# Batches in pairs: 32-row class products, a ring of seven PSUM banks, and fp16 row products in a fused layernorm and graph-convolution kernel

## What is computed

```python
def reference(x, adj, L0_gnn_b1, L0_gnn_b2):
    h = jnp.maximum(_layernorm(x, axis=-1), 0.0)
    return x + _L0_gnn_ref(h, adj, L0_gnn_b1, adj, L0_gnn_b2)

def _construct_adj(x, k):              # k = 8
    fv = x.mean(axis=1)
    nf = fv / jnp.linalg.norm(fv, axis=1, keepdims=True)
    sim = nf[:, :, None] * nf[:, None, :]
    _, idx = jax.lax.top_k(sim, k + 1)
    idx = idx[..., 1:]
    adj = jnp.zeros((Bn, Nn, Nn), x.dtype).at[b_ix, r_ix, idx].set(1.0)
    adj = jnp.maximum(adj, jnp.swapaxes(adj, 1, 2))
    return adj.at[:, d, d].set(1.0)

def _gc(x, adj, W, b):
    deg = adj.sum(axis=2, keepdims=True)
    h = x @ W.T + b
    return jnp.einsum('bij,bjh->bih', adj / deg, h)
```

## Time and profile before

| engine | busy us | share of the span |
|---|---|---|
| PE | 448.8 | 90% |
| DVE | 413.3 | 83% |
| ACT | 297.4 | 59% |
| POOL | 205.9 | 41% |

### The profile page before, as it was taken

How to read it: one execution, slowest core, us unless ns; L and a number is a source line. 1 busy time by engine, 2 the same in 40 slices (tenths; PEclk the granted TensorE clock), 3 DMA queues, 4 the chain that set the end, 5 groups by cost and what they waited for, 6 DMA issues and landing times.

```text
span 500.3 us, 7423 instructions
## 1 busy us (share of the span) xinstructions
PE 448.8 (90%) x2188; PEld 201.7 (40%) x2188; DVE 413.3 (83%) x742; ACT 297.4 (59%) x633; POOL 205.9 (41%) x873
## 2 busy tenths in 40 slices
PE   0645599896998999999999999999999999999996
PEld 0112244343343444444444444444444444444442
DVE  5999879997899997999799989999799747953363
ACT  3975576747785477776767477657767552114300
POOL 2626464703547136623736345613644342314100
PEclk9986789999899999999999999999999999999999
DMA  8990000158202690059302970159104400350035
GB/s 312 368 376 1 1 1 2 74 205 285 110 1 84 234 352 5 1 195 349 130 1 86 305 284 0 73 198 342 64 0 168 170 1 1 126 211 1 0 128 209
DMA packets 19401, 68.21 MB, mean 136 GB/s; under 512 B 1824, under 2 KB 2464, under 8 KB 19360
## 3 DMA queue, kind: packets, MB, share of 16 engines
q1 hardware_dynamic: 19360, 67.73, 36.5%
HBM read 34.17 MB, written 33.55 MB: 135 GB/s over the span
## 4 chain that ended last, share of the span: by engine, by line
PE 35%; DVE 35%; issue 10%; ACT 8%; POOL 8%; POOLq 2%; DMA 1%; SPq 0%; DVEq 0%; ACTq 0%
PE ps L394 28%; DVE bn L955 7%; DVE hl L977 6%; DVE hl L983 5%; DVE xs L996 5%; PE ps L406 4%; POOL gat L759 4%; ACT hf L569 3%; ACT hl L578 3%; POOLq L756 2%; DVE idx L1019 2%; DVE fv L1011 1%; ACT hl L590 1%; DVE kind L1028 1%; DVE fv L1023 1%
## 5 line engine op out<-in xcount | busy, mean ns | idle before, releaser
L394 PE MATMUL ps<-hl,wh 128*128 128x512 f16 x1024 | 308.9, 384 | 23.1 <-DVE wl L1152 11.3
L394 PE MATMUL ps<-hl,wl 128*128 128x512 f16 x512 | 196.1, 383 | 0.0
L394 PEld LDWEIGHTS ps<-hl,wh 128*128 128x128 f16 x1024 | 98.1, 99 | 148.9 <-issue 18.0
L569 ACT ACTIVATE hf<-xs,nbias,rstd 128x1024 f32<-128x1024 f32 x64 | 79.0, 1234 | 52.3 <-POOL nbias L745 47.1
L590 ACT ACTIVATE hl<-ps 128x512 f16<-128x512 f32 x128 | 74.8, 591 | 56.7 <-PE ps L406 56.6
L983 DVE SCALAR_TENSOR_TENSOR hl<-ps,hl 128x1024 f16<-128x1024 f32 x64 | 77.7, 1214 | 29.6 <-ACT hl L590 29.3
L977 DVE TENSOR_TENSOR hl<-hf,hl 128x1024 f16<-128x1024 f32 x64 | 77.5, 1213 | 21.8 <-ACT hl L578 21.6
L996 DVE SCALAR_TENSOR_TENSOR xs<-ps,sc,xs 128x1024 f32<-128x1024 f32 x62 | 77.8, 1266 | 5.9 <-PE ps L406 5.7
L394 PEld LDWEIGHTS ps<-hl,wl 128*128 128x128 f16 x512 | 50.6, 99 | 61.9 <-issue 2.7
L955 DVE BATCH_NORM_STATS2 bn<-xs 128x6 f32<-128x512 f32 x104 | 66.7, 679 | 4.6 <-DMA xs<-x_dram 4.5
L578 ACT ACTIVATE hl<-hf 128x1024 f16<-128x1024 f32 x64 | 67.6, 1057 | 1.9
(11 more groups left out here) (135 smaller groups left out, 450.9 us busy)
## 6 DMA issues: line engine op xcount, KB each, us to landing
xs<-x_dram SPq DMA_DIRECT2D x62, 512.0 KB, 6.9
out_dram<-xs SPq DMA_DIRECT2D x31, 1024.0 KB, 4.8
xs<-x_dram SPq DMA_DIRECT2D x4, 256.0 KB, 3.4
out_dram<-xs SPq DMA_DIRECT2D x4, 256.0 KB, 2.1
wt<-adj_t_dram SPq DMA_DIRECT2D x1, 256.0 KB, 10.5
b1r<-b_row_dram SPq DMA_DIRECT2D x1, 128.0 KB, 10.7
b2r<-b_row_dram SPq DMA_DIRECT2D x1, 128.0 KB, 11.6
cs<-consts_dram SPq DMA_DIRECT2D x1, 86.5 KB, 10.3
```

The costliest lines, as they stand in the source:

```text
L394: pe.matmul(ps[i % 3][:, m], w[:, k, o], hl[:, slot, part, k, cols], start=(k == 0 and w is wh and part == 0), stop=False)
L569: act.activation(hf[:, c % NHF], xs[:, n % NX, k], ACT.Relu, bias=nbias[:, n % RB, k:k + 1], scale=rstd[:, n % RB, k:k + 1], accum_out=s_a ...
```

## The change

Seven things change together.

1. **Order of units.** Units come in pairs of two batches: `PAIRED` is (lane 0, half 0), (lane 1, half 0), (lane 0, half 1), (lane 1, half 1), then the same for lanes 2 and 3. Layer 2 of the last group uses `LAST`. Semaphore counts follow (`turn`, `both`).
2. **Class rows.** `rows` takes a pair. Weight and moving operand are the lane's own 32 partitions of `lw` and `onehot`; m runs outside, the two units inside. The masked copies (`l1w`, `l2w`, `C_MINE`, L1093) are gone, and PE waits on `row_w`.
3. **PSUM.** One tensor `ps` of seven banks, used one bank at a time round the ring (bank (2i+m) mod 7 for place i), with one wait per bank. Where a unit's banks are 6 and 0, `y_lo` and `final` are two instructions of 512 columns (`pieces`). The means go to `pm`.
4. **Row products.** `q1r` and `q2` are fp16 high and low parts, and `plain_rows` and `times_q2` become `pair_product`: six fp16 matmuls of 256 columns with `wh` and `wl` instead of two in fp32. POOL makes the parts: one more operation in `plain_q1`, and in `late_sums` one multiplication, two copies and two subtractions in place of two multiplications.
5. **PE order.** `rows` of a pair after both `main`; `means` after the second and third pair; `class_sizes` ahead of the last `rows`.
6. **ScalarE order** from group 1 on: both halves of `make_h` for `front(g,0)` ahead of the first `y_hi`; one half of `front(g,1)` ahead of the second pair's `y_hi`, after `class_values`; the rest as in the diff.
7. **VectorE order** from group 1 on, as in the diff.

```diff
             def main(layer, n, half):
-                if i >= 3:
-                    was, m, h = unit_of_place(i - 3)
-                    pe.wait_ge(lo2_ready if was == 1 else done, NH * m + h + 1)
...
                 for m in range(KC):
+                    was = (KC * i + m - RING) // KC
+                    if was >= 0:
+                        of = unit_of_place(was)
+                        pe.wait_ge(lo2_ready if of[0] == 1 else done, turn(*of))
...
-            def rows(layer, n, half):
-                if half == 0:
-                    pe.wait_ge(l1w_ready if layer == 1 else l2w_ready, GB * g + LANE[n] + 1)
...
+            def rows(*them):
+                layer, g = them[0][0], GROUP[them[0][1]]
+                pe.wait_ge(row_w, 2 * g + layer)
+                pe.wait_ge(onehot_ready, g + 1)
+                for m in range(KC):
+                    for layer, n, half in them:
+                        at = slice(LANE[n] * LANES, (LANE[n] + 1) * LANES)
+                        last = pe.matmul(bank(place(layer, n, half), m), lw[at, layer - 1, m * P:(m + 1) * P],
+                                         onehot[at, g % 2, half * HALF:(half + 1) * HALF], start=False, stop=True)
+                        if m == KC - 1:
+                            last.then_inc(l1_ps if layer == 1 else l2_ps, 1)
...
+            def pair_product(q):
+                for k in range(KC):
+                    for part, w in ((0, wh), (0, wl), (1, wh)):
+                        last = pe.matmul(pm_r, q[:, part, k].rearrange("p b c -> p (b c)"), w[:, k],
+                                         start=(k == 0 and part == 0 and w is wh), stop=(k == KC - 1 and part == 1))
+                last.then_inc(row_ps, 1)
...
             for g in range(1, NG):          # ScalarE
                 make_h(n, 0)
+                make_h(n, 1)
                 y_hi(*us[0][1:])
-                make_h(n, 1)
                 y_hi(*us[1][1:])
                 root(FIRST[g] + 8)
                 class_values(g)
-                for u in us[2:]:
-                    y_hi(*u[1:])
+                n = front(g, 1)
+                make_h(n, 0)
+                y_hi(*us[2][1:])
+                y_hi(*us[3][1:])
...
                 make_h(n, 0)                # n = front(g, 3)
-                make_h(n, 1)
                 if is_group(g + 1):
                     class_count(g + 1)
                     split_rows(2 * (g + 1))
+                make_h(n, 1)
                 root(FIRST[g] + 11)
...
             for g in range(1, NG):          # VectorE
                 if g > 1:
+                    final(*unit(g - 1, 14)[1:])
                     final(*unit(g - 1, 15)[1:])
                 stats(first + 8, 0)
                 h_lo(n, 0)
-                y_lo(*us[0][1:])
                 stats(first + 8, 1)
                 mean_var(first + 8)
                 h_lo(n, 1)
-                y_lo(*us[1][1:])
+                y_lo(*y[0])
+                y_lo(*y[1])
                 root_inverse(first + 8)
                 stats(first + 9, 0)
-                y_lo(*us[2][1:])
+                n = front(g, 1)
+                h_lo(n, 0)
                 stats(first + 9, 1)
                 mean_var(first + 9)
-                y_lo(*us[3][1:])
+                y_lo(*y[2])
+                y_lo(*y[3])
...
                 if to:
                     rows_w(2 * (g + 1))
-                final(*us[1][1:])
-                root_inverse(first + 11)
                 h_lo(n, 1)
                 if to:
                     class_degrees(g + 1)
                     inverse_degrees(g + 1)
-                final(*us[2][1:])
+                root_inverse(first + 11)
```

More of the change, by code:

```diff
@@ L48 @@
 ROOM = 2.0 ** 14
+SHRINK = 16.0
 CLASS_WANT = (1, -2, 0, -3)
@@ L170, in gnn_kernel @@
         lw = sb("lw", [P, 2, S], BF16)
[L171 to L175 removed]
+        ps = ctx.enter_context(nc.psum_tensor("ps", [P, RING, HALF], F32))
         pm = ctx.enter_context(nc.psum_tensor("pm", [P, HALF], F32))
@@ L272, in front, with order @@
             return n if n < stop else None
+        def order(g, layer):
+            return LAST if g == NG - 1 and layer == 2 else PAIRED
         def unit(g, i):
@@ L290, in unit_of_place, with bank, pieces, banks @@
             return unit(g, i - 2 * NH * FIRST[g])
+        def bank(i, m):
+            return ps[:, (KC * i + m) % RING]
+        def pieces(i):
+            first = KC * i % RING
+            return [(0, 1), (1, 2)] if first == RING - 1 else [(0, KC)]
+        def banks(i, piece):
+            first = (KC * i + piece[0]) % RING
+            return ps[:, first:first + piece[1] - piece[0]]
         def means_bank(g, half):
-            return pm if half == 1 and g < 2 else pf
+            return ps[:, RING - 1] if g == 0 and half == 1 else pm[:]
         def on_scalar(n):
@@ L436, in plain_rows @@
                     pe.wait_ge(fv_copied, NH)
-                for k in range(KC):
-                    last = pe.matmul(pm_r, q1r[:, k].rearrange("p b c -> p (b c)"), wt[:, k],
-                                     start=(k == 0), stop=(k == KC - 1))
-                last.then_inc(row_ps, 1)
+                    pe.wait_ge(w_ready, 1)
+                pair_product(q1r)
             def times_q1(g):
@@ L476, in _ @@
             for g in range(NG):
[L477 to L489 removed]
+                us = units(g, 0) + units(g, 1)
@@ L490, in _ @@
+                for i in range(0, len(us), 2):
+                    for u in us[i:i + 2]:
+                        if g > 0 or us.index(u) >= EARLY:
+                            main(*u)
+                    rows(*us[i:i + 2])
+                    if i == (2 if g == 0 else 0):
+                        times_q1(g)
+                    if g > 0 and i in (2, 4) and is_group(g + 1):
+                        means(g + 1, i // 2 - 1)
+                us = units(g, 2) + units(g, 3)
                 if g == 0:
@@ L491, in _ @@
                     means(1, 0)
+                main(*us[0])
+                if g == 0:
                     means(1, 1)
-                third = units(g, 2)
-                for u in third[:2]:
-                    main(*u)
+                main(*us[1])
                 times_q2(g)
-                for u in third[2:3]:
-                    main(*u)
-                for u in third[:3]:
-                    rows(*u)
-                for u in third[3:]:
-                    main(*u)
-                    rows(*u)
@@ L504, in _ @@
-                fourth = units(g, 3)
-                for u in fourth[:1]:
-                    main(*u)
-                    rows(*u)
+                main(*us[2])
+                rows(*us[:2])
+                main(*us[3])
+                rows(*us[2:4])
                 if is_group(g + 1):
+                    main(*us[4])
+                    main(*us[5])
+                    rows(*us[4:6])
                     plain_rows(g + 1)
-                for u in fourth[1:3]:
-                    main(*u)
-                    rows(*u)
@@ L513, in _ @@
-                if is_group(g + 1):
+                    main(*us[6])
+                    main(*us[7])
                     class_sizes(g + 1)
-                for u in fourth[3:]:
-                    main(*u)
-                    rows(*u)
+                    rows(*us[6:])
+                else:
+                    for u in us[4:]:
+                        main(*u)
+                        rows(u)
         @block.scalar
@@ L995, in final @@
                     return
-                dve.scalar_tensor_tensor(xs[:, n % NX, :, cols], ps[place(2, n, half) % 3][:], scal(S_C2),
-                                         xs[:, n % NX, :, cols], ALU.mult, ALU.add).then_inc(done, 1)
+                for piece in pieces(i):
+                    ms = slice(*piece)
+                    last = dve.scalar_tensor_tensor(xs[:, n % NX, ms, cols], banks(i, piece), scal(S_C2),
+                                                    xs[:, n % NX, ms, cols], ALU.mult, ALU.add)
+                last.then_inc(done, 1)
             def top_a(g):
@@ L1320, in _ @@
                 mean_var(first + 10)
-                final(*us[0][1:])
+                final(*end[0])
+                final(*end[1])
                 h_lo(n, 0)
                 root_inverse(first + 10)
-                final(*us[1][1:])
-                h_lo(n, 1)
+                final(*end[2])
                 if to:
@@ L1328, in _ @@
                     u_sums(g + 1)
-                final(*us[2][1:])
+                final(*end[3])
                 if to:
@@ L1332, in _ @@
                     kinds(g + 1)
-                final(*us[3][1:])
-                n, us = front(g, 3), units(g, 3)
-                if to:
                     classes(g + 1)
-                final(*us[0][1:])
+                h_lo(n, 1)
+                final(*end[4])
+                n = front(g, 3)
                 if to:
```

194 lines of the change are left out of this document (91 added, 103 removed).

## The result

The changed kernel takes 514.78 us, the median of four runs (512.52 to 515.39), against 502.44 us for the kernel before in the same comparison: a ratio of 1.0235 (interval 1.0211 to 1.0258). It is slower by 12 us; 509 was forecast. The profiled execution took 514.36 us with a span of 512.5 us, 12.2 more than the span before.

A forecast was written before the change was run, and what follows sets the result against it. PE was taken as the bound, VectorE close behind. Five steady groups at +1.8, group 6 at -1.2, group 7 at -0.9 and group 0 at 0 sum to +6.9 on 502.07: 509.0 us, range 489 to 519.

The forecast's parts named there:

- 32-row rows, 0.63 a pair: Four 32-row matmuls of a pair on PE take 0.63 us instead of 0.86, saving 1.9 us per group.
- The rival that they don't overlap: Row tiles on PE run one after another, 1.06 us for a pair, time 522 us; chance 0.1.
- fp16 products, 0.65 each: Each row product on PE takes 0.65 us as six fp16 matmuls instead of 0.86; two per group save 0.4.
- Walk of the steady group: Steps through one group, applied to groups 1 to 5: period 56.35 us against 54.55, 1.8 us more each.
- place 5: Unit in the third pair, counted from 0; PE waits 2.45 us there for the third y_lo.
- place 3: Unit in the second pair, counted from 0; PE waits 0.75 us there for the first y_lo.
- Groups 6 and 7: The last two groups get shorter: group 6 by 1.2 us, group 7 by 0.9.
- Group 1 as a steady group: Group 1 was given the steady form of groups 1 to 5, so 1.8 us more.
- Group 0: The opening group: saved copies and rows stand against a waiting third y_hi; taken as 0, between -2 and +2 us.
- The prediction's own sign of being wrong: A gain or loss of more than 4 us outside the steady groups, in group 0 or the tail.
- The faster rival: The order does not bite and PE's list decides: steady group 51.5 us, time 483, reaching to 492; chance 0.2.

The follow-up runs named there:

- the mended order: The changed kernel with third y_hi first, root_inverse(first+11) earlier, and the second half of make_h(front(g,0)) behind the first two y_hi: 493.16 us, ratio 0.9836.
- after: The changed kernel, unaltered, as measured and profiled against the kernel before: 514.78 us, ratio 1.0235.
- the third `y_hi` first: The changed kernel with third and fourth y_hi ahead of make_h's first half for front(g,1), VectorE's list to match: 500.73 us, ratio 0.9962.
- The repeated run: The changed kernel with root_inverse(first+11) alone moved earlier, profiled once more without alteration: 506.93 us, one execution.

## Why the prediction was right, and where it was off

The forecast was slower by 7 us through the order of the lists. The order does cost what makes the change lose: with it mended the same work is 18.6 us faster and below the kernel before. But the +6.9 was not made up as forecast, and that the time came out within 6 us of it is in part luck. By its steps:

- *32-row rows, 0.63 a pair*: measured 0.63 (0.54 and 0.09 ahead of it). The rival that they don't overlap is refuted by the timeline, and the saving of 1.9 us per group by 1.8 between the two forms in the mended order.
- *fp16 products, 0.65 each*: measured 0.67. Their price on POOL was seen as a wait of 0.65 for `q2`; it was 0.28 in after, because the group is late by then, and 1.35 in the mended order. They buy nothing.
- *Walk of the steady group*: with time 0 at 235.17, `nbias` was forecast at 5.2 (4.85 measured), first `y_hi` at 9.8 (9.5), `root_inverse` at 13.6 (13.3), `make_h` done at 17.95 (17.6), third `y_lo` done at 21.85 (21.65). The wait at place 5 was forecast at 2.45 and is 2.35. The smaller waits were put too high (`q1` 0.9 against 0.53, place 3 0.75 against 0.55), and PE's list too low: 55.63 less 3.9 of waits is 51.7, not 50.9 (the list left out `class_sizes`, 0.13 us, and had `times_q1` at 0.84 where it takes 1.0). A period of 56.35 was forecast, 55.63 measured; the step against before was forecast at 1.8 and is 0.8 to 1.1 where the clock held.
- *Groups 6 and 7*: forecast -2.1 together, measured -2.6.
- *Group 1 as a steady group*: in the sum at +1.8, measured -0.4. Its place 3 had a wait of 3.24 us before already, with the 1.2 GHz level behind it, and the same order that costs 0.55 in a steady group made it 6.25. But the wait for the masked copies (0.96) is gone and those for `xs` fell from 1.45 to 0.35, so its waits rose by only 2.2 us (5.65 to 7.86), less than the work that PE is spared. I had taken the steady form for groups 1 to 5 and not walked group 1.
- *Group 0*: the term that was mis-sized most. It was in the sum at 0, between -2 and +2, and is +7.8. Of these 2.1 us lie ahead of PE's first `main`. No run shows whether the change causes them: there is one trace of the kernel before (43.1), and the kernels built on the change start `main` anywhere from 42.6 to 45.2. Behind it are 5.7 us, 4.0 of them waits. The wait for `lw` rose from 1.85 to 4.32 us through the one bank for both means, and PE waits 2.79 us for `h_lo` ahead of the first means, where it waited for nothing; the prediction named neither. The remaining 1.7 go with the clock: from about 80 us to the group's end the granted clock was 1.00 before and 0.91 after. In the traces of the kernels that leave group 0 as the change made it, these 72.8 us range from 69.5 (granted clock 0.92) to 74.7 (0.82).
- *The clock*: not in the sum at all. Groups 4 and 5 lost 1.8 us each by it.

The difference of 5.3 us between +6.9 and +12.2 is made up of group 0 (+7.8), group 1 (-2.2), groups 4 and 5 (+0.8 and +1.1, with +1.8 each of clock in them), groups 2 and 3 (-0.7 and -1.0) and groups 6 and 7 (-0.5). The steady mechanism was therefore seen rightly and priced too high: groups 1 to 5 were forecast at +9.0 and measured at +7.0, of which 3.6 is clock. Group 0 filled the gap by luck. The prediction's own sign of being wrong, a loss outside the steady groups of more than 4 us that "would be group 0 or the tail", came true for group 0, and that 514.8 lies within the range of 489 to 519 is owed to its width. The faster rival, 483 us where PE's list decides, named the right point (the third `y_hi`), but the changed kernel doesn't reach it. With both lists mended it takes 493.2 at a period of 52.8 to 52.9; the 484.9 of the last version needed the edits to groups 0 and 1 and the fp32 products besides.

## What to carry to other kernels

When a list is rewritten for larger steps (here pairs), each call that waits for another engine's result and stands ahead of a call on PE's path costs its whole wait in every repetition; look for it in the list before looking at totals. A saving that is paid for by a mode or a setup pays only where enough work shares it: 32-row products save 0.23 us for a pair and lose 0.21 for a single unit. And walk the opening and the first repetition by themselves. Group 0, put at nothing, was 7.8 of the 12.2 us, and in group 1 a wait of the steady form was ten times as long.

## What the runs showed of the hardware that was not expected

After a wait of 2.4 us PE went on at full clock in some groups and fell in others. The timeline of PE and the windows of after around such a wait in group 4, and a window of group 3 for comparison:

```profile
312.64 0.60 PE L423 MATMUL ps<-hl,wh 128*128 128x512 f16 x2 [2.42 <-DVE hl L1017]
313.08 0.55 PE L423 MATMUL ps<-hl,wl 128*128 128x512 f16 x1
313.43 1.06 PE L423 MATMUL ps<-hl,wh 128*128 128x512 f16 x2
...
314.84 1.03 PE L434 MATMUL ps<-onehot,lw 32*128 32x512 bf16 x4
```

```profile
312.50:314.50 2.00, 1.86 (x6) 0.60 (x6) 2.00 (x5) 1.54 (x3) 1.69 (x8) 0.67 0.00 0
314.50:317.00 2.50, 2.50 (x21) 0.52 (x20) 1.59 (x2) 1.09 (x4) 2.09 (x6) 0.58 0.01 3
257.00:259.00 2.00, 2.00 (x18) 0.64 (x20) 2.00 (x4) 1.43 (x4) 1.68 (x9) 1.00 0.00 0
```

The granted clock goes to 0.67 and 0.58 of full speed as a mean of the window, a mixture of the levels 2.4 and 1.2 GHz, and the matmuls double their distance some 0.5 us after work began again; it costs 1.6 to 1.8 us. With the wait gone (the third `y_hi` first) no steady group fell. The repeated run shows that the same wait in the same kernel falls in one execution and not in another. Why after fell twice in the same two groups isn't settled. The Trainium skill ("TensorE: Matmul & The Clock Gate", Part 1) says that the number of matmuls at the slower level when a kernel starts varies between runs of the same kernel. These groups lie in the middle of the kernel, which the sentence doesn't speak of; there the two profiles of one kernel, with none and with two steady groups fallen, vary too.
